# Attention scores of a two-layer block: 48 stacked rows in place of 64, and the row maxima subtracted by a 49th row instead of a one-hot product

## The reference

```python
query = split(norm(x) @ w_q.T + b_q)      # 16 heads, d = 16
key   = split(ctx @ w_k.T + b_k)
value = split(ctx @ w_v.T + b_v)
scores = einsum('bhqd,bhkd->bhqk', query, key) / sqrt(16)
scores = where(mask == 0, -1e9, scores)   # the mask is all ones in these inputs
attn = exp(scores - max(scores)) / sum(...)
out  = (attn @ value) merged @ w_o.T + b_o
x = x + tanh(g_xattn[1]) * out
```

## Time and profile before

| | |
|---|---|
| median of 3 runs | 1747.3 us (1745.95 to 1748.33) |
| the profiled execution's own time | 1748.64 us |
| span of its profile, first to last instruction | 1746.9 us |
| mean granted TensorE clock | 0.970 of full speed |
| PE busy, of the span | 1607.0 us (92%) |
| DVE busy | 1368.7 us (78%) |
| ACT busy | 1056.6 us (60%) |
| POOL busy | 942.5 us (54%) |

### The profile page before, as it was taken

How to read it: one execution, slowest core, us unless ns; L and a number is a source line. 1 busy time by engine, 2 the same in 40 slices (tenths; PEclk the granted TensorE clock), 3 DMA queues, 4 the chain that set the end, 5 groups by cost and what they waited for, 6 DMA issues and landing times.

```text
span 1746.9 us, 42800 instructions
## 1 busy us (share of the span) xinstructions
PE 1607.0 (92%) x14411; PEld 1258.5 (72%) x14411; DVE 1368.7 (78%) x3213; ACT 1056.6 (60%) x1894; POOL 942.5 (54%) x1329
## 2 busy tenths in 40 slices
PE   5999999999999992677999999999999999999997
PEld 4888888888888882444777777767777777767666
DVE  5688888888888866768888888888888888887642
ACT  6666666666666553255656666665666666565654
POOL 5555666566655635224556465555646465564535
PEclk9999999999999996688999999999999999999999
DMA  6322212221122002342323232332223232333200
GB/s 211 101 62 74 76 60 60 74 76 60 60 73 77 7 1 71 96 123 78 83 81 91 78 96 74 90 86 83 80 84 91 74 94 79 86 85 86 62 15 20
DMA packets 215099, 133.59 MB, mean 76 GB/s; under 512 B 45937, under 2 KB 214257, under 8 KB 214769
## 3 DMA queue, kind: packets, MB, share of 16 engines
q1 hardware_dynamic: 215024, 132.61, 26.1%
HBM read 101.07 MB, written 25.17 MB: 72 GB/s over the span
## 4 chain that ended last, share of the span: by engine, by line
PE 42%; ACT 8%; issue 6%; DVE 3%; SPq 1%; POOL 1%; DMA 0%; ACTq 0%; POOLq 0%
PE b_bank L1637 23%; PE b_bank L1716 7%; PE b_scoreT L1694 4%; PE b_score L1677 3%; PE b_scoreT L1698 3%; ACT L31 3%; ACT b_E L1275 2%; ACT b_Y L1335 2%; PE b_bank L1645 1%; ACT b_xT L1281 1%; PE b_bank L1731 1%; DVE b_nm L1457 1%; SPq L1086 0%; SPq L1097 0%; PE b_scoreT L1662 0%
## 5 line engine op out<-in xcount | busy, mean ns | idle before, releaser
L1457 DVE TENSOR_REDUCE b_nm<-b_score 128x4 bf16<-128x1024 f32 x256 | 314.5, 1228 | 121.1 <-PE b_score L1677 115.2
L1275 ACT ACTIVATE b_E<-b_scoreT 128x1024 f32<-128x1024 f32 x256 | 262.2, 1024 | 191.1 <-PE b_scoreT L1698 190.3
L1199 POOL TENSOR_SCALAR b_YT<-b_Y 128x512 bf16<-128x512 f32 x128 | 85.9, 671 | 292.0 <-ACT b_Y L1335 282.5
L760 PE MATMUL bank<-W2T,G 128*128 128x256 f32 x1024 | 231.2, 379 | 0.0
L760 PEld LDWEIGHTS bank<-W2T,G 128*128 128x128 f32 x1024 | 192.1, 190 | 24.8
L31 ACT ACT_TABLE_LOAD x156 | 200.1, 1283 | 9.8 <-PEq L875 6.4
L1335 ACT ACTIVATE b_Y<-b_bank,b1f 128x256 f32<-128x256 f32 x256 | 107.5, 471 | 160.0 <-PE b_bank L1637 159.6
L1637 PE MATMUL b_bank<-b_hT,f 128*128 128x256 bf16 x1536 | 189.9, 274 | 11.4 <-ACT b_Y L1335 11.4
L1637 PE MATMUL b_bank<-f,b_YT 128*128 128x256 bf16 x1536 | 184.0, 273 | 2.5 <-POOL b_YT L1202 1.6
L727 PE MATMUL bank<-hT,W1T 128*128 128x256 bf16 x1536 | 178.3, 273 | 6.4 <-ACT G L497 2.5
L1637 PEld LDWEIGHTS b_bank<-b_hT,f 128*128 128x128 bf16 x1536 | 143.3, 98 | 54.7 <-ACT b_Y L1335 19.7
(11 more groups left out here) (209 smaller groups left out, 3455.6 us busy)
## 6 DMA issues: line engine op xcount, KB each, us to landing
b_Q<-q_dram SPq DMA_DIRECT2D x256, 64.0 KB, 2.5
b_K<-k_dram SPq DMA_DIRECT2D x256, 64.0 KB, 2.5
xin<-in_x SPq DMA_DIRECT2D x32, 256.0 KB, 4.5
ctxn<-in_ctx SPq DMA_DIRECT2D x32, 256.0 KB, 2.8
mask_in<-in_mask SPq DMA_DIRECT2D x32, 256.0 KB, 3.0
X<-in_x SPq DMA_DIRECT2D x32, 256.0 KB, 4.4
ctxt<-in_ctxT SPq DMA_DIRECT2D x32, 256.0 KB, 4.6
b_ctxt<-in_ctxT SPq DMA_DIRECT2D x32, 256.0 KB, 2.8
```

Of the source, the lines that this page charges most:

```text
L760: last = nc.tensor.matmul(out_ps[:, t], G[w.parity][:, h, t * P:(t + 1) * P], W2T[:, h], start=h == 0, stop=h == HC - 1)
L1275: nc.scalar.activation(E[:, pair:pair + 2], scoreT_ps[:, :, :, :], ACT.Exp).then_inc(sig["E"], 1)
L1457: nc.vector.tensor_reduce(pair, score_ps[:, :, :, :], AX.X, ALU.max, negate=True).then_inc(sig["nm"], 1)
```

## The change

The fourth product of parts (low by low) is left out of the stack: the three pairs of `TERMS` take 48 rows of each half (`TOP` = 48). SP issues 6 DMAs in place of 8 for each stack. Row 48 of each half of `K4` is set to one at the start by POOL, where the one-hot matrix was built before. Row 48 of each half of `Q4` receives the negated maxima: once both transposes of `nm` have landed, SP copies rows 0 to 7 of each half of `nmT` into that one row, one DMA for each half (`row_of_maxima`). `scores` multiplies over 48 rows, `scores_transposed` over 49 rows, and its second matmul is gone; `scores_transposed(0)` now waits for the two copies.

```diff
+    TOP = len(TERMS) * DK
-        one_hot = sb("one_hot", [P, NP, P], BF16)
                 def stack_keys():
                     sp.wait_ge(sig[f"kspill{q.parity}"], landed(q))
+                    if at_batch(q, 0):
+                        sp.wait_ge(sig["ones_set"], 5)
...
-                        for r in range(4):
+                        for r, (_, part) in enumerate(TERMS):
...
-                                         k_dram[q.parity][r // 2].rearrange("(h e d) n -> e d h n", e=2, d=DK)[odd]).then_inc(
+                                         k_dram[q.parity][part].rearrange("(h e d) n -> e d h n", e=2, d=DK)[odd]).then_inc(
...
+                def row_of_maxima():
+                    sp.wait_ge(sig[f"nmT{m.parity}"], landed(m, per=T))
+                    sp.sem_inc(sig["row_ready"], 1)
+                    for odd in range(2):
+                        row = odd * HALF + TOP
+                        sp.dma_start(Q4[m.parity][row:row + 1, :, :],
+                                     nmT[m.parity][odd * HALF:odd * HALF + NP, :]).then_inc(sig[f"top{m.parity}"], 16)
...
                 if m:
                     transpose_maxima()
+                    row_of_maxima()
...
-                    nc.gpsimd.memset(one_hot[:, :, :], 0.0).then_inc(sig["ones_set"], 1)
-                    pool.wait_ge(sig["ones_set"], 4)
-                    for odd in range(2):
-                        nc.gpsimd.affine_select(out=one_hot[:, :, :], in_=one_hot[:, :, :], compare_op=ALU.not_equal, fill=1.0,
...
+                    for i in range(2):
+                        nc.gpsimd.memset(K4[i][:, :, :], 1.0).then_inc(sig["ones_set"], 1)
...
                 def scores(i):
-                            rows = slice(odd * HALF, (odd + 1) * HALF)
+                            rows = slice(odd * HALF, odd * HALF + TOP)
...
                 def scores_transposed(i):
                     if i == 0:
-                        pe.wait_ge(sig[f"nmT{a.parity}"], landed(a, per=T))
+                        pe.wait_ge(sig[f"top{a.parity}"], landed(a, per=2))
...
-                            rows = slice(odd * HALF, (odd + 1) * HALF)
-                            nc.tensor.matmul(scoreT_ps[:, odd, k], K4[a.parity][rows, i, tile(k)],
-                                             Q4[a.parity][rows, i, :], start=True, stop=False)
-                        for odd in range(2):
-                            rows = slice(odd * HALF, (odd + 1) * HALF)
-                            last = nc.tensor.matmul(scoreT_ps[:, odd, k], one_hot[rows, i, :], nmT[a.parity][rows, :],
-                                                    start=False, stop=not mask)
+                            rows = slice(odd * HALF, odd * HALF + TOP + 1)
+                            last = nc.tensor.matmul(scoreT_ps[:, odd, k], K4[a.parity][rows, i, tile(k)],
+                                                    Q4[a.parity][rows, i, :], start=True, stop=not mask)
```

More of the change, by code:

```diff
@@ L999, in phase_b, with at_batch @@
         bank = {i: scope.enter_context(nc.psum_tensor(f"b_bank{i}", [P, 2, 256], F32)) for i in range(6, 10)}
+        def at_batch(b, k):
+            return b is not None and isinstance(b.number, int) and b.number == k
         def whole_bank(i):
@@ L1094, in stack_queries @@
                     for odd in range(2):
-                        for r in range(4):
+                        for r, (part, _) in enumerate(TERMS):
                             rows = slice(odd * HALF + r * DK, odd * HALF + (r + 1) * DK)
                             sp.dma_start(Q4[q.parity][rows, :, :],
-                                         q_dram[q.parity][r % 2].rearrange("(h e d) n -> e d h n", e=2, d=DK)[odd]).then_inc(
+                                         q_dram[q.parity][part].rearrange("(h e d) n -> e d h n", e=2, d=DK)[odd]).then_inc(
                                 sig[f"qstack{q.parity}"], 16)
@@ L1319, in values_copy @@
                     act.wait_ge(sig["V_mm"], done(q))
-                    act.wait_ge(sig["ones_set"], 6)
+                    act.wait_ge(sig["ones_set"], 5)
                     if (due := done(q, back=2, per=NH // HG)) is not None:
@@ L1452, in maxima @@
                     if i == 0:
-                        dve.wait_ge(sig["ones_set"], 6)
+                        dve.wait_ge(sig["ones_set"], 5)
                         if (due := landed(m, back=1, per=T)) is not None:
@@ L1667, in scores @@
                     if i == 0:
-                        pe.wait_ge(sig[f"kstack{m.parity}"], landed(m, per=8))
-                        pe.wait_ge(sig[f"qstack{m.parity}"], landed(m, per=8))
+                        pe.wait_ge(sig[f"kstack{m.parity}"], landed(m, per=6))
+                        pe.wait_ge(sig[f"qstack{m.parity}"], landed(m, per=6))
                         if mask:
@@ L1685, in scores_transposed @@
                     if i == 0:
-                        pe.wait_ge(sig[f"nmT{a.parity}"], landed(a, per=T))
-                        pe.wait_ge(sig["ones_set"], 6)
+                        pe.wait_ge(sig[f"top{a.parity}"], landed(a, per=2))
+                        pe.wait_ge(sig["ones_set"], 5)
                         pe.wait_ge(sig["b1f"], 1)
```

3 lines of the change are left out of this document (removed).

## The result

| | before | after |
|---|---|---|
| median of 4 executions, us | 1746.68 | 1708.36 |
| lowest and highest, us | 1745.95 to 1748.33 | 1701.08 to 1709.88 |
| profiled execution: time, span, us | 1748.64, 1746.9 | 1701.08, 1699.2 |

The changed kernel takes 0.9771 of the time before (95% interval 0.9742 to 0.9800): 2.3% faster. Forecast were 1704.5 us and 1696 to 1728.

A forecast was written before the change was run, and what follows sets the result against it. PE, busy 92% of the span, was taken to set the pace. 27 periods x 1.40 = 37.8 plus 5.0 gave 42.8 us off 1748.64, so 1705.8; the median being 1.3 lower, 1704.5 us, range 1696 to 1728.

The forecast's parts named there:

- The one-hot product: In `scores_transposed(1)` to `(7)`, dropping it saves PE 1.54 us a period; at `(0)` nothing, behind the wait for `exponential(0)`.
- The cost read from the pace: On PE's timeline, eight matmuls take 0.44 us and four 0.22, so each `scores_transposed` saves 0.22 us.
- The group's 127.4 us: Busy time of the one-hot product's 1024 matmuls on PE, which the prediction said is not what it costs.
- The margins: At PE's hand-overs with other engines, little room is left; 0.14 us taken off, leaving 1.40 us a period.
- 48 and 49 rows: In both score products, fewer rows than 64 leave the matmul pace unchanged: 0 gain.
- The copy: Ahead of `scores_transposed(0)`, the maxima land 2.5 us after the second issue (bounds 2.2 and 5.7), costing 0.
- the cover of 0.63: At `scores_transposed(0)`, PE can start 0.63 us late before `scores_transposed(1)` moves; landing up to 2.69 us after issue is free.
- The rival that the copy lands late: At `scores_transposed(0)`, landing after 3.3 us loses 0.61 us a period, 16.5 in all: 1721 us; chance 0.14.
- SP and POOL: SP is free at 1012.9, ahead of the context load: 0; POOL's set-up at the start: 0, at most 2 us.
- The 26 and the rest: Over the whole run, 27 periods of 1.40 us give 37.8, other iterations 5.0: together 42.8 us off.
- The five other iterations: Three at the start and two at the end, taken at 1.0 us gain each (between 0 and 1.76): 5.0 us.
- The next bound: DVE, at 89% of a 28.9 us period, and ACT hand-overs take half the gain: 1723 us; chance 0.13.

The follow-up runs named there:

- four matmuls more at 4: Changed kernel with four extra matmuls, their result overwritten, in `scores_transposed(4)`: 1710.5 us, 0.9799 of the kernel before.
- four more at 0: Changed kernel with four extra matmuls, their result overwritten, in `scores_transposed(0)`: 1707.53 us, 0.9774 of the kernel before.
- the three terms alone: Changed kernel with the one-hot product kept and no copies of the maxima, so only 48 rows and six stack DMAs: 1745.88 us, 0.9982 of the kernel before.
- one hop more: Changed kernel with the maxima copied first to a scratch tile, then into the queries' row: 1784.08 us, 1.0196 of the kernel before.
- the three profiles: Profiles of the changed kernel: its first measurement (median 1708.36 us) and two repeats without edit (1702.47 and 1702.87 us).
- both moves: Changed kernel with `scores(1)` ahead of `scores_transposed(1)` and `scores(7)` ahead of `hidden(1)`: 1701.71 us, 0.9734 of the kernel before.
- The filled wait: Changed kernel with 44 unread matmuls in PE's wait for the copies in the last batch: 1702.50 us, 0.9739 of the kernel before.

## Why the prediction was right

**The one-hot product: right.** The cost read from the pace (0.22 us for four) holds, in the changed kernel's rows and in the kernel with four matmuls more at 4: +0.22. That nothing of it counts at `scores_transposed(0)` is shown by the four more at 0: +0.00. That the dropped product is the whole gain of a period is shown from both sides: with three terms and the product the period is 30.36, and without product and copies 28.78. The group's 127.4 us would have promised some three times the gain that came.

**The margins: mis-sized.** I took 0.14 off 1.54. The measured 1.52 is 7 x 0.22 within 0.02; no hand-over took anything back, so this term was too small by 0.12 x 26 = 3 us. `maxima(3)` did turn late, as foreseen, and that cost nothing visible.

**48 and 49 rows: right.** Pace and duration are unchanged, and the three terms alone are worth 0.2% at most.

**The copy: right, with two terms mis-sized that cancel in part.** Landing took 1.75 us, below my lower bound of 2.2; the second copy is issued 0.76 behind the first, not 0.46. The copy arrives 7.84 us after the start of `scores(7)` (1029.63 - 1021.79), not 8.20 (1014.46 - 1006.26), which left PE a wait of 0.19 (0.23 in the other kind of period) and not 0.44 at `(0)`. Each was a size and not a step of the argument: the cover of 0.63 was there and was not used up. The Trainium skill (DMA: Bandwidth & Descriptors, Rules for kernel authors) says that a transfer under 64 KB pays mostly overhead, from which the prediction took it that 4 KB last as long as 64 KB. The trace agrees in the direction only: 4 KB land after 1.75 us and a 64 KB piece of a stack after 2.5, and since one comes from SBUF and the other from DRAM, these rows don't tell how much of the difference is due to the bytes. The rival that the copy lands late was a live one: one hop more, 2.55 us, makes the kernel slower than before.

**SP and POOL: right.** SP is done with the store at 1029.23 and issues the context load at 1029.79, so the copies don't hold it. POOL's two memsets end at 685.2, and the first stack of keys, which waits for them, goes out at 706.7.

**The 26 and the rest.** 27 x 1.40 + 5.0 = 42.8 was forecast off the profiled span; 39.6 + 5.6 + 2.5 = 47.7 came in that execution, 39 in the longest of them. The five other iterations were the softest term, and they are what spreads. I gave them 1.0 each as a fixed gain; the three profiles show 8.1, 6.3 and -0.3 us for start and tail together, against the one profile before. The smallest goes with the most time at the clock's lower level: in the tail, apart from the last 3 us, none in the first two and 10.2 us in the third. The median of all thirteen executions is 1702.87, 1.6 us from the forecast; the first four's 1708.36 holds three of the long ones. That the forecast lies so near is in part luck: the periods gave 3 us more than was taken for them, and start and tail, which no term of the sum describes by its clock, gave less in the longer executions.

**The next bound: half right.** That DVE stands close behind was named as a rival for the gain. It took nothing from this change, but it ends the next one: of 0.77 us of waits for ACT (0.44 in the mean and 0.33) only 0.15 came with both moves.

**Open:** what decides, from one execution to the next, whether the clock falls in the last batches. The wait for the copies is not enough for it (2.65 us in the first profile, without a fall) and not needed for it (the run without copies). The longer tails go with more time at the lower level: 106.5 to 107.3 us with at most 3.4 us of it, 110.9 with 10.2, 113.3 (four more at 0) with 17.1 and 112.5 (both moves) with 20.5. Why it comes is not shown. The filled wait had five executions under 1705, but the intervals of all these versions overlap. Open too: what the hop costs in the first and last iterations. The version with `scores(1)` first and the last wait filled has the lowest median, 1700.45; that it beats the changed kernel is not shown by more than its period of 28.67 against 28.78.

## What to carry to other kernels

Price matmuls that are removed by the distance of starts in the timeline and not by a group's busy time, and count only those behind which no wait of another engine absorbs the gain. A hop that is hidden is priced by its deadline: work out the time at which it begins to count, and expect nearly the whole lateness in every period from there on, perhaps with time at a lower clock on top. Where executions of one kernel differ by more than the effect, compare the period, which repeated here within 0.02 us, and not the total.

## What was not expected of the hardware

- PE's granted clock fell again and again in a phase in which PE was busy 90% of the time: in the kernel with one hop more, stretches of 3.4 or 6.8 us at half the clock began in waits of 2.5 to 3.3 us or (once) 1.1 us behind one, once in a period: 0.91 over 200 us, and 17 us lost over the 26 periods. Later in the same execution waits of 2.4 to 2.5, and two of 3.06 and 3.34, left it at 1.00. In the run without copies it fell with no wait longer than 0.90 us in the 35 us before.
- A copy of 8 x 512 bytes within SBUF into one partition landed 1.75 us after its issue, sooner than 64 KB from memory (2.5), while SP was busy with its issue for 0.70 us (1.39 / 2), against 0.45 for a piece of the stack (2.69 / 6).
